# A two-attention, two-expert-layer kernel on Trainium2: the score pairs for the row maxima lead the exponentials by 36 heads in place of 28

## The chip, the cores and the metric

The kernel runs on one core of one Trainium2 chip. The metric is the device time of one execution in microseconds (us), as the median of several. All work of the core is done by TensorE (PE, matrix products), VectorE (DVE), ScalarE (ACT), GpSimd (POOL) and the DMA engines, which the queue of SyncE (SP) feeds here. Each of them has an instruction stream of its own, written by hand, and they meet at semaphores: an instruction that waits holds up everything behind it in its own stream, and nothing else.

## The reference, cut to what matters

The model applies four residual layers to x, which is 16 batches of 128 tokens by 256 features: a cross-attention with 16 heads of 8 features, an expert layer with 64 experts, an mLSTM-like attention, and a transformer block with its own attention and four experts. Only the first is touched:

```
q = split_heads(layernorm(x)^T @ Wq^T + bq)      # 16 batches, 16 heads, 256 positions, 8 features
k = split_heads(ctx^T @ Wk^T + bk)
v = split_heads(ctx^T @ Wv^T + bv)
attn = softmax(q @ k^T / sqrt(128))               # 256 x 256 for each batch and head
out = attn @ v, heads joined, @ Wo^T + bo
x = x + tanh(g_xattn[0]) * out
```

Positions are the 256 features of x, and the 128 tokens are what the projections mix. So there are 16 x 16 = 256 heads in all, counted through from batch 0, head 0.

## The kernel before, in words

The first attention is `layer0_attention`, with one function for each engine. The projections come first, two batches at a time. Each projected q and k is cut into three bf16 parts, written to HBM (L132), and read back as a "stack" of one batch: `a_qs` holds 72 rows (9 part pairs of 8 features) by 16 heads by 256 positions, `a_ks` the same for the keys. A product over these 72 rows gives a score of nearly fp32 accuracy. `stack(b)` of `layer0_sp` (L135) issues the six DMAs of one batch, three for q (L146) and three for k (L147), of 192 KB each. The stacks lie in a ring of `A_RING` = 4, so stack b + 4 overwrites stack b, and before it is issued SP waits until PE is through with the exponentials' pairs of batch b (L144). Stacks 0 to 3 are loaded with no such wait.

Each head is multiplied twice. `score_max` (L195) makes the scores with the queries on the partitions (two matmuls, L204), and DVE reduces them to the negated row maxima (L423). When a batch's 16 heads are reduced, `max_to_rows` turns the 128x32 tile of maxima with a transpose (L214), ACT copies it (L327, L328), POOL cuts it into three bf16 parts (L474 to L478), and SP writes these as three more rows of the query stack with three small DMAs (`max_rows`, L150 to L154). Then `exponentials` (L223) makes the scores again with the keys on the partitions, now over 75 rows, so that the maximum is already subtracted (L232), and ACT takes the exponential (L340). For every four heads `times_v` (L246) multiplies by v and by ones, `normalise` turns the sums back (L256), and once a batch `to_features` and `residual` (L265, L270) do the output projection.

The order of the work is a loop over `A_STEPS` steps of two heads, the same in every engine's function. Ahead of it, PE runs `AHEAD` heads of `maxima` alone. In the loop, head i of the exponentials is preceded by head i + `AHEAD` of the maxima (L278). The transpose of a batch's maxima follows two heads behind the batch's last head (L218 to L220). ACT (L350 to L355) and DVE (L437 to L445) follow the same count. SP's stream is in L162 to L171: first the max rows that fall into the first `AHEAD` heads, then a loop over the steps that issues `max_rows` where the count reaches a batch's end, and `stack` at the end of each eighth step. SP does not compute, so its loop only fixes an order; each entry goes when its own semaphore allows it and all entries ahead of it are gone.

With `AHEAD` = 28, `max_rows(0)` is issued ahead of the loop. In it the order is `max_rows(1)` (step 2), `stack(4)` (step 7), `max_rows(2)`, `stack(5)`, `max_rows(3)`, and so on. PE needs stack 4 at head 64 of the maxima, which stands ahead of head 36 of the exponentials, and turns the maxima of batch b ahead of exponentials' head 5 of batch b - 1.

Of the kernel before, what the change touches and what calls it, by code (L numbers as in the profile page):

```python
# [71 lines left out]
HEADS, HD = 16, 8  # L72
# [9 lines left out]
A_SLOTS = 3  # L82
A_RING = 4
A_EXPS = 8
AHEAD = HEADS + 3 * HEADS // 4
A_STEPS = NB * A_PAIRS + 6


# [23 lines left out]
def layer0_sp(k, m, s, ring):  # L112
# [22 lines left out]
    def stack(b):  # L135
        r, i = b % A_RING, b // 2
        flat = lambda t, first, count: t[first * HD:(first + count) * HD, :, :].rearrange("p h n -> p (h n)")
        parts_of = lambda n: io[f"a_{n}_parts"][b].rearrange("t (d h) n -> t d (h n)", d=HD)
        sp.wait_ge(ring["q_out"][i % A_SLOTS], 2 * DMA * (i // A_SLOTS + 1))
        sp.wait_ge(ring["k_out"][i % A_SLOTS], 2 * DMA * (i // A_SLOTS + 1))  # L140
        if b < A_RING:
            sp.wait_ge(s.k_ones, b + 1)
        else:
            sp.wait_ge(s.exp_scores, (b - A_RING + 1) * HEADS)  # L144
        for t in range(3):
            sp.dma_start(flat(m.qs[r], 3 * t, 3), parts_of("q")[t].unsqueeze(0).broadcast_to([3, HD, HEADS * POS])).then_inc(ring["stack_in"][r], DMA)  # L146
            sp.dma_start(flat(m.ks[r], 3 * t, 3), parts_of("k")).then_inc(ring["stack_in"][r], DMA)  # L147
# [12 lines left out]
    for b in range(1, A_RING):  # L160
        stack(b)
    for i in range(AHEAD):  # L162
        if i >= 2 and (i - 2) % HEADS == HEADS - 1:
            max_rows((i - 2) // HEADS)
    for n in range(A_STEPS):
        for h in range(2):
            i = 2 * n + h + AHEAD - 2
            if i % HEADS == HEADS - 1 and i // HEADS < NB:
# [5 lines left out]
def layer0_pe(k, m, s, ring):  # L174
# [41 lines left out]
    def maxima(i):  # L216
        if i < NB * HEADS:
            score_max(*divmod(i, HEADS))  # L218
        b, h = divmod(i - 2, HEADS)
        if h == HEADS - 1 and 0 <= b < NB:  # L220
            max_to_rows(b)
# [50 lines left out]
    pe.wait_ge(k.ident_ready, 1)  # L272
    for i in range(AHEAD):
        maxima(i)
    for n in range(A_STEPS):
        b, j = divmod(n, A_PAIRS)
        for h in (2 * j, 2 * j + 1):
            maxima(b * HEADS + h + AHEAD)  # L278
            if b < NB:
# [11 lines left out]
def layer0_act(k, m, s, ring):  # L291
# [38 lines left out]
    def maxima(i):  # L330
        b, h = divmod(i - 2, HEADS)
        if h == HEADS - 1 and 0 <= b < NB:
            max_to_rows(b)
# [15 lines left out]

    for i in range(AHEAD):  # L350
        maxima(i)
    for n in range(A_STEPS):
        b, j = divmod(n, A_PAIRS)
        for h in (2 * j, 2 * j + 1):
            maxima(b * HEADS + h + AHEAD)  # L355
            if b < NB:
# [1937 lines left out]
```

## Time and profile before

| what | us |
|---|---|
| median of 3 runs | 1828.59 (1820.28 to 1829.84) |
| the profiled execution's own time | 1817.43 |
| its span | 1816.1 |
| PE busy, share of the span | 1606.5 (88%) |
| DVE busy | 1259.6 (69%) |
| ACT busy | 1019.4 (56%) |
| POOL busy | 765.8 (42%) |
| projections and first stacks | 0 to 111 |
| loop of the first attention | 111 to 350.4 |
| the other three layers | 350.4 to 1816.1 |

An engine's busy time is the sum of its instructions' times; PE's is modelled at the ends of matmuls, so a busy PE need not be at its peak. The last three lines come from the timeline of instructions: the first exponential pair starts at 110.93, and the first layer's last residual ends at 350.4. The granted clock of a stretch is given as a share of TensorE's full speed: 1.00 is 2.4 GHz, 0.50 is 1.2 GHz.

### The profile page before, as it was taken

The numbers are of one execution on the slowest core, as the hardware profiler recorded it, in microseconds if no ns is written. First come the engines' busy times: TensorE is split into PE (matmuls) and PEld (weight loads), VectorE is DVE, ScalarE is ACT, GpSimd is POOL, SyncE is SP. The second block draws the span as 40 slices with busy tenths as digits, with TensorE's granted clock in tenths as the row PEclk, the third lists the DMA queues.
The fourth block names the chain that finished last, engine by engine and source line by source line (L and its number), as shares of the span: only waits on it lengthen the run. The fifth ranks groups of instructions, "written<-read, shape, count | busy, mean of one in ns | idle before, by whom it ended". The sixth has DMA issues, their size and how long they took to land.

```text
span 1816.1 us, 30483 instructions
## 1 busy us (share of the span) xinstructions
PE 1606.5 (88%) x10932; PEld 1268.4 (70%) x10932; DVE 1259.6 (69%) x2321; ACT 1019.4 (56%) x2050; POOL 765.8 (42%) x575
## 2 busy tenths in 40 slices
PE   4379999789999999999986964899899999999898
PEld 2135555368888888888872533788787778888687
DVE  6458788378644455444445576999999999999454
ACT  4247777644433335333335653877776877677453
POOL 5200000024435333333330014798798688877000
PEclk9569899899999999999996987999999999999899
DMA  5613232243343333343400002123112111211220
GB/s 155 154 55 83 76 84 61 80 111 105 94 129 106 104 110 102 108 116 102 118 10 6 4 2 92 48 72 103 56 56 68 56 56 56 68 48 30 70 47 24
DMA packets 73349, 137.42 MB, mean 76 GB/s; under 512 B 12824, under 2 KB 41308, under 8 KB 70384
## 3 DMA queue, kind: packets, MB, share of 16 engines
q1 hardware_dynamic: 73200, 135.48, 26.4%
q8 instruction: 88, 1.44, 0.3%
q14 instruction: 61, 0.50, 0.1%
HBM read 125.70 MB, written 8.95 MB: 74 GB/s over the span
## 4 chain that ended last, share of the span: by engine, by line
PE 54%; DVE 19%; issue 9%; DMA 8%; ACT 6%; POOL 2%; SPq 1%; DVEq 0%; ACTq 0%; POOLq 0%
PE bank L67 13%; PE bank L69 13%; PE bank L68 13%; DMA a_qs<-a_mparts 5%; DVE b_straight L1938 3%; DVE b_straight L1892 2%; PE bank L246 2%; PE bank L232 2%; PE bank L204 2%; ACT b_turned L1809 2%; DVE b_peak L1909 2%; POOL e_hidden L944 1%; DVE b_probs L1907 1%; PE bank L1700 1%; PE bank L1732 1%
## 5 line engine op out<-in xcount | busy, mean ns | idle before, releaser
L944 POOL TENSOR_TENSOR e_hidden<-e_gated,e_comb_wide 128x512 f32<-128x512 f32 x132 | 211.0, 1599 | 346.7 <-DVE e_gated L909 331.1
L784 ACT CAST e_hidden_hi<-e_hidden 128x512 fp32r<-128x512 f32 x132 | 82.0, 622 | 320.6 <-POOL e_hidden L944 320.6
L902 DVE TENSOR_TENSOR e_hidden_lo<-e_hidden,e_hidden_hi 128x512 fp32r<-128x512 f32 x132 | 98.2, 744 | 209.8 <-ACT e_hidden_hi L784 209.8
L423 DVE TENSOR_REDUCE a_negmax<-bank 128x2 f32<-128x512 f32 x256 | 165.6, 684 | 64.6 <-PE bank L204 63.3
L69 PE MATMUL bank<-e_x_hi,e_weights_lo 128*128 128x512 f32 (+1 forms) x528 | 209.5, 397 | 0.0
L67 PE MATMUL bank<-e_x_hi,e_weights_hi 128*128 128x512 f32 (+1 forms) x528 | 208.4, 395 | 0.7 <-ACT e_comb_rows L744 0.7
L68 PE MATMUL bank<-e_x_lo,e_weights_hi 128*128 128x512 f32 (+1 forms) x528 | 208.4, 395 | 0.0
L1809 ACT ACTIVATE b_turned<-bank,b_swap_bias 64x512 f32<-64x512 f32 x256 | 174.9, 683 | 17.7 <-PE bank L69 12.9
L1996 POOL TENSOR_TENSOR b_turned<-b_turned,b_rope 128x512 f32<-128x512 f32 x128 | 167.5, 1329 | 5.3 <-ACT b_turned L1809 4.8
L340 ACT ACTIVATE a_exp<-bank 128x512 f32<-128x512 f32 x256 | 142.9, 596 | 42.8 <-PE bank L232 35.4
L69 PE MATMUL bank<-e_weights_hi,e_hidden_lo 128*128 128x256 f32 (+1 forms) x528 | 149.4, 283 | 0.0
L67 PE MATMUL bank<-e_weights_hi,e_hidden_hi 128*128 128x256 f32 (+1 forms) x528 | 148.2, 281 | 0.5 <-DVE e_hidden_lo L902 0.5
L68 PE MATMUL bank<-e_weights_lo,e_hidden_hi 128*128 128x256 f32 (+1 forms) x528 | 148.4, 281 | 0.0
L1938 DVE TENSOR_TENSOR b_straight<-b_straight,b_turned 128x512 f32<-128x512 f32 x128 | 140.5, 1136 | 0.0
L1798 ACT ACTIVATE b_probs<-b_probs,b_peak_scaled 128x128 f32<-128x128 f32 x256 | 99.7, 391 | 68.2 <-DVE b_peak_scaled L1911 68.1
L204 PE MATMUL bank<-a_ks,a_qs 72*128 72x256 bf16 x512 | 108.0, 297 | 31.0 <-DMA a_ks<-a_k_parts 13.2
L1978 POOL TENSOR_TENSOR b_qk_lo<-b_raw_qk,b_qk_hi 128x512 fp32r<-128x512 f32 x64 | 84.7, 1324 | 109.9 <-DVE b_qk_hi L1872 109.9
L909 DVE TENSOR_TENSOR e_gated<-e_silu,bank 128x512 f32<-128x512 f32 x132 | 90.5, 686 | 56.7 <-PE bank L69 44.2
L232 PE MATMUL bank<-a_qs,a_ks 75*128 75x256 bf16 x512 | 100.2, 280 | 21.0 <-DMA a_qs<-a_mparts 20.1
L69 PEld LDWEIGHTS bank<-e_x_hi,e_weights_lo 128*128 128x128 f32 (+1 forms) x528 | 98.7, 187 | 22.7
L67 PE MATMUL bank<-b_x_hi,b_qk_hi 128*128 128x512 f32 x256 | 103.0, 402 | 12.8 <-POOL b_qk_lo L1978 4.5
L67 PEld LDWEIGHTS bank<-e_x_hi,e_weights_hi 128*128 128x128 f32 (+1 forms) x528 | 99.4, 188 | 19.7 <-ACT e_comb_rows L744 1.1
(326 smaller groups left out, 4318.1 us busy)
## 6 DMA issues: line engine op xcount, KB each, us to landing
e_comb_wide<-e_combT SPq DMA_DIRECT2D x130, 256.0 KB, 4.0
e_raw<-in_e_weights SPq DMA_DIRECT2D x64, 384.0 KB, 4.5
b_raw_qk<-in_b_wqk SPq DMA_DIRECT2D x64, 256.0 KB, 2.8
a_qs<-a_q_parts SPq DMA_DIRECT2D x48, 192.0 KB
a_ks<-a_k_parts SPq DMA_DIRECT2D x48, 192.0 KB
b_raw_v<-in_b_wv SPq DMA_DIRECT2D x16, 512.0 KB, 3.8
b_raw_o<-in_b_wo SPq DMA_DIRECT2D x64, 128.0 KB, 2.0
moe_comb_wide<-b_comb_rows SPq DMA_DIRECT2D x16, 256.0 KB, 6.7
```

Of the source, the lines that this page charges most:

```text
L67: pe.matmul(out, w_hi, x_hi, start=start, stop=False, skip_group_check=True)
L68: pe.matmul(out, w_hi, x_lo, start=False, stop=False, skip_group_check=True)
L69: return pe.matmul(out, w_lo, x_hi, start=False, stop=stop, skip_group_check=True)
L204: last = pe.matmul(bank[:, qb * POS:(qb + 1) * POS], m.qs[r][0:TERM_ROWS, h, qb * P:(qb + 1) * P], m.ks[r][0:TERM_ROWS, h, :], start=True, ...
L232: last = pe.matmul(bank[:, kb * POS:(kb + 1) * POS], m.ks[r][0:ROWS, h, kb * P:(kb + 1) * P], m.qs[r][0:ROWS, h, :], start=True, stop=True)
L340: act.activation(m.expo[at % A_EXPS][:, :, :].rearrange("p k q -> p (k q)"), banks[2 + h % 2][:, :], ACT.Exp, scale=float(1 / np.sqrt(np.f ...
L423: dve.tensor_reduce(m.negmax[b % 2][:, h, :], banks[h % 2][:, :].rearrange("p (q n) -> p q n", q=2), AX.X, ALU.max, negate=True).then_inc( ...
L944: pool.tensor_tensor(m.hidden[i][0:rows, :], m.gated[i][0:rows, :], m.comb_wide[u % E_RING][0:rows, chunk * BANK:(chunk + 1) * BANK], ALU. ...
L1798: last = act.activation(w.probs[n % 3][:, b, :], w.probs[n % 3][:, b, :], ACT.Exp, scale=SCALE, bias=w.peak_scaled[i][:, b:b + 1], accum_o ...
L1809: last = act.activation(w.turned[i][dst:dst + half, which, :], banks[bank][src:src + half, :], ACT.Identity, bias=m.swap_bias[dst:dst + ha ...
L1938: dve.tensor_tensor(w.straight[n % 2][:, which, :], w.straight[n % 2][:, which, :], w.turned[n % 2][:, which, :], ALU.add).then_inc(s.rotated)
L1996: pool.tensor_tensor(x, x, w.rope[:, 1, :].unsqueeze(1).to_broadcast([P, CHUNK, S]), ALU.mult).then_inc(s.qk_sine)
```

## The change

One constant:

```
-AHEAD = HEADS + 3 * HEADS // 4
+AHEAD = 2 * HEADS + HEADS // 4
```

`AHEAD` goes from 28 to 36. PE, ACT and DVE now run 36 heads of the maxima ahead of the loop, and exponentials' head i is preceded by maxima head i + 36; the last 36 exponential heads have no maxima beside them, where it was 28. `max_rows(0)` and `max_rows(1)` are issued by SP ahead of its loop. In the loop the order becomes `max_rows(2)` (step 6), `stack(4)` (step 7), `max_rows(3)`, `stack(5)`, and so on. PE needs stack 4 ahead of exponentials' head 28, which is head 12 of batch 1. The maxima of batch b are turned ahead of exponentials' head 13 of batch b - 2. The rings, tiles, instructions and waits stay as they are, as does their number.

## Rows read from the trace of the kernel before

**Rows 1.** Window: its length; busy (instructions) of PE, PEld, DVE, ACT, POOL; clock; DMA; GB/s.
```profile
125.70:323.00 197.30, 187.18 (x1871) 111.90 (x1869) 157.40 (x333) 152.19 (x319) 14.50 (x39) 0.97 0.28 75
```

**Rows 2.** Waits of PE, 90 to 620 us: total us, times, longest.
```profile
PE bank L232 <- DMA a_qs<-a_mparts: 20.1, 11, 10.0
PE bank L204 <- DMA a_ks<-a_k_parts: 13.2, 1, 13.2
```

**Rows 3.** Waits of PE, 125 to 323 us.
```profile
PE bank L232 <- DMA a_qs<-a_mparts: 10.1, 10, 2.1
```

**Rows 4.** Timeline of SP's queue: start, us, what is issued.
```profile
125.74 0.74 SPq L146 DMA_DIRECT2D a_qs<-a_q_parts  x1
...
139.57 0.76 SPq L146 DMA_DIRECT2D a_qs<-a_q_parts  x1
...
146.82 1.83 SPq L153 DMA_DIRECT2D a_qs<-a_mparts  x3
...
218.39 0.75 SPq L146 DMA_DIRECT2D a_qs<-a_q_parts  x1
```

**Rows 5.** Windows around the transfers of stacks 4 and 10 (last two: DMA share, GB/s).
```profile
128.00:131.50 3.50, 3.50 (x37) 2.09 (x37) 2.82 (x6) 2.90 (x8) 0.67 (x2) 1.00 0.71 157
131.50:135.00 3.50, 3.50 (x38) 2.10 (x37) 2.82 (x6) 2.85 (x6) 0.45 (x2) 1.00 0.24 76
...
139.50:140.50 1.00, 0.45 (x4) 0.11 (x2) 0.97 (x4) 0.61 (x2) 0.00 (x0) 1.00 0.01 2
...
232.00:232.50 0.50, 0.50 (x5) 0.18 (x3) 0.50 (x2) 0.50 (x2) 0.00 (x0) 1.00 0.03 3
```

**Rows 6.** Timeline of PE at full clock, batches 0 and 2: start, us, matmuls.
```profile
123.07 0.39 PE L204 MATMUL bank<-a_ks,a_qs 72*128 72x256 bf16 x2
...
139.56 0.39 PE L204 MATMUL bank<-a_ks,a_qs 72*128 72x256 bf16 x2
140.91 0.39 PE L232 MATMUL bank<-a_qs,a_ks 75*128 75x256 bf16 x2 [0.97 <-DMA a_qs<-a_mparts]
...
143.93 0.38 PE L204 MATMUL bank<-a_ks,a_qs 72*128 72x256 bf16 x2
...
144.67 0.28 PE L214 MATMUL bank<-ident,a_negmax 128*32 128x128 f32 x1
...
151.18 0.38 PE L204 MATMUL bank<-a_ks,a_qs 72*128 72x256 bf16 x2
...
153.86 0.39 PE L232 MATMUL bank<-a_qs,a_ks 75*128 75x256 bf16 x2
...
154.32 0.39 PE L204 MATMUL bank<-a_ks,a_qs 72*128 72x256 bf16 x2
```

**Rows 7.** Timeline of PE around its longest wait in the loop.
```profile
198.18 0.39 PE L204 MATMUL bank<-a_ks,a_qs 72*128 72x256 bf16 x2
200.70 0.61 PE L232 MATMUL bank<-a_qs,a_ks 75*128 75x256 bf16 x2 [2.13 <-DMA a_qs<-a_mparts]
...
206.03 0.64 PE L204 MATMUL bank<-a_ks,a_qs 72*128 72x256 bf16 x2
...
207.31 0.42 PE L214 MATMUL bank<-ident,a_negmax 128*32 128x128 f32 x1
...
209.92 0.61 PE L204 MATMUL bank<-a_ks,a_qs 72*128 72x256 bf16 x2
...
218.38 0.39 PE L204 MATMUL bank<-a_ks,a_qs 72*128 72x256 bf16 x2
```

**Rows 8.** Window behind that wait.
```profile
200.20:210.40 10.20, 9.70 (x60) 4.83 (x61) 3.85 (x7) 4.72 (x10) 1.11 (x3) 0.50 0.34 99
```

**Rows 9.** Timeline of the loop's end: exponential heads 228 and 246, last residual.
```profile
322.88 0.39 PE L232 MATMUL bank<-a_qs,a_ks 75*128 75x256 bf16 x2
...
336.68 0.61 PE L232 MATMUL bank<-a_qs,a_ks 75*128 75x256 bf16 x4
...
349.93 0.48 DVE L451 SCALAR_TENSOR_TENSOR resid<-a_proj,gates,resid 128x256 f32<-128x256 f32 x1 [3.05 <-ACT a_proj L369]
```

## The prediction

> **What bounds the kernel now.** Only the first attention's loop is touched, 111 to 350.4 us, so I read its window first. From 125.7 to 323 us PE is busy for 187.2 of 197.3 us, DVE for 157, ACT for 152; the DMA engines carry 75 GB/s at a mean share of 0.28 [rows 1]. PE is the bound there, short of 10 us. The list of waits says what these are: ten times PE stood before an exponential pair (L232) for the max rows' DMA, 10.1 us together, 2.1 at the longest [rows 3]. An eleventh, 10.0 us, is the one ahead of the first exponential, and before that PE waits once, 13.2 us, for a key stack [rows 2].
>
> That the max rows are late is worth a second look, because they are tiny. The reader is to see in SP's timeline that their DMAs (146.82) go out behind the six large ones of a stack (139.57) [rows 4]. The windows show what these large ones do: 157 GB/s at a share of 0.71 for some 3.5 us, then only 75 GB/s at 0.24, which is some four of 16 engines, for 8 us more, and traffic stops near 139.5 to 140.5 for stack 4, issued at 125.74 [rows 4, 5]. The max rows queued behind it release PE at 140.91 [rows 6]. Stack 10 is issued at 218.39 and its traffic has all but ended at 232 [rows 4, 5]. So a stack takes 13.6 us (232.0 less 218.4) to 15.2 us (140.91 less 125.74) from issue to use; I take 14.3, what it takes to the middle of the window 139.5 to 140.5. That is about as long as a whole batch takes on PE: from 139.56 to 154.32 is 14.8, less 1.1 of wait, 13.6 us [rows 6]. The DMA path of the stacks is nearly as full as PE, although the mean share of 0.28 hides it. This decides the case, since no stack is waited for in the loop today.
>
> **The change, part by part.**
>
> *The lead over the max rows.* The transpose of a batch's maxima comes eight heads earlier against the exponentials that need it, 19 heads ahead in place of 11. With 13.6 / 16 = 0.85 us a head that is 6.8 us more, against waits of 2.1 at most [rows 3]: all ten go, 10 us. With them goes the low clock behind the longest. That wait is 200.70 - 198.18 - 0.2 = 2.3 us, the clock granted behind it is 0.50 (1.2 GHz) from 200.2 to 210.4 [rows 8], and this batch lasts 218.38 - 198.18 = 20.2 us, so 20.2 - 13.6 - 2.3 = 4.3 us are lost to the clock [rows 7]. Together some 14 us.
>
> *Eight more heads ahead of the loop.* They fall into PE's wait of 10.0 us before the first exponential [rows 2], which ends with the landing of max rows 0, issued ahead as before; eight score pairs cannot take more than eight whole heads of the loop, 6.8 us. Were stack 2, which the last four need, late by more than the 3 us left, its lateness would be added. At the other end eight heads leave the loop at 0.85 us and are done alone at (336.68 - 322.88) / 18 = 0.77 [rows 9]: about 0.7 us gained, inside the sum below. The transpose of the maxima now follows the output projection (L270) by one head and waits for ACT to have copied it from the same bank; that costs at most a few tenths a batch, and lies inside the next wait.
>
> *The stacks' deadline.* Stack b + 4 may be issued only after exponentials' head 15 of batch b, in both kernels. Its first use was 20 heads later and is now 12. At full clock 12 heads are 151.18 - 139.56 - 1.1 = 10.5 us [rows 6], where the transfer wants 14.3. A wait of nearly 4 us is new, in each batch, on L204. Being in PE's stream, it also holds the exponential pairs behind it, then ACT and `times_v`, hence head 15 and the issue of the next stack: the wait closes a loop.
>
> *SP's order.* `max_rows(b + 2)` now stands immediately ahead of `stack(b + 4)` in SP's stream, and its maxima are turned at head 13. From head 12's score pair to the transpose are 144.67 - 143.93 = 0.74 us, from there through ACT and POOL to SP 146.82 - 144.67 = 2.15, and the three issues take 1.83 [rows 4, 6]. So the stack goes out 4.8 us behind head 12, where head 15 would allow it at 154.32 - 151.18 = 3.1 [rows 6]. Push: 1.7 us. The max rows themselves are small and don't slow the stack by more than I can read.
>
> **The sum.** With the wait in the loop, a batch lasts from one stack's landing to the next: head 12 to stack issue, plus 14.3. At full clock that is 4.8 + 14.3 = 19.1. But the wait is then 19.1 - 13.6 = 5.5 us, more than the one behind which the clock fell [rows 7, 8]. At 1.2 GHz a head's two pairs take 0.85 ((207.31 - 206.03) / 3 = 0.43 a pair), from head 12 to head 14 it is 209.92 - 206.03 = 3.9 us and the end of head 15 comes 2.0 later, at 5.9 [rows 7]; the push is hidden (1.28 + 2.2 + 1.8 = 5.3). The batch is 5.9 + 14.3 = 20.2. PE's work in it is 13.6 + 4.3 = 17.9, so 2.3 us of wait stay, just what made the clock fall before: the low clock keeps itself alive. I take 20.2.
>
> Start: batch 0 runs as now, with head 13 at 123.07. Plus 0.2 to the transpose, 2.15, 1.83 and a tenth: stack 4 goes out at 127.4 (now 125.74) and lands at 141.7. Stacks 5 to 15 are eleven periods: 11 x 20.2 = 222.2, so stack 15 lands at 363.9, at head 12 of batch 12. Behind it are 16 heads with maxima, 17.9 us, then 36 heads alone: the present end from head 228, 350.4 - 322.9 = 27.5, plus 8 x 0.77 = 6.1 [rows 9]. 363.9 + 17.9 + 27.5 + 6.1 = 415.4, against 350.4: **65 us more**. What follows the first attention starts from its last residual and does not change. From the profiled execution's 1817.4 that gives 1882; the timed runs shown lie 3 to 12 us above that execution, so I put the forecast at 1886.
>
> **A rule that speaks against it.** The rows show a transfer at 157 and then 75 GB/s [rows 5]. The Trainium skill, "DMA: Bandwidth & Descriptors" (Specifications), puts the HBM limit of one core at about 358 GB/s. By it 1.18 MB would take an estimated 3.3 us, and the stack would be there in time; the rows contradict it for these patterns. The same page (Rules for kernel authors) says that an outermost dimension smaller than 16 confines a DMA to that many engines. The key loads have an outermost 3, so it speaks for a rate that does not recover when the queue is otherwise free. No row shows which engines carried them.
>
> **Rivals.**
> (a) Faster: a stack is quicker once no max rows mix into its tail, and lands within 10.5 - 1.7 = 8.8 us. For it: the two do share the tail now. Against: traffic in the tail is 75 GB/s over 8 us, 600 KB, and three max rows are 24 KB. Then the gains alone count: 1817.4 - 14 - 1 = 1802. The page's HBM limit would lead here. 4%.
> (b) In between: transfers near 10 us, period 14.8, as now: within 0.5%. 3%.
> (c) The wait without a lasting low clock: period 19.1. 141.7 + 210.1 + 13.6 + 33.6 = 399.0, 49 us more: 1866. The clock window of a 2.3 us wait is one case only. 25%.
> (d) My forecast, 20.2: 1886, 65%.
> (e) The order on SP hurts more than computed, for instance because the large issues back up the queue, or the transfer takes 15.2 throughout: 11 x 21.1 more, 76 us: 1893, with the spread of the runs 1905. 3%.
> That the constant does nothing is excluded; it moves instructions in four streams.
>
> **Range and chances.** Lowest: transfer 13.6, full clock: 141.0 + 11 x 18.4 + 47.2 = 390.6, 40 us more, 1857. Highest: (e), 1905. Slower by over 0.5% (what a measurement of this kernel can tell from no change, 9 us): 0.93; within: 0.03; faster: 0.04.
>
> **What would show it.** In the changed kernel PE's waits should list L204 on the DMA of `a_ks` or `a_qs` twelve times, some 2 to 6 us each, and L232 on `a_mparts` once. SP should issue the first q load of a stack 1.9 us behind the first max row, and one such set each 19 to 20.5 us. The clock should be 0.50 for about half of each batch from 142 us on. The attention's end should stand near 415. Wrong it is if stacks land in under 10.5 us, or if the waits of L204 are on anything but a stack; the step I trust least is whether the low clock returns in every batch.

## The result, and the profile after

| | before | after |
|---|---|---|
| median, us | 1824.43 (1818.83 to 1829.84, 4 runs) | 1889.78 (1879.73 to 1901.54, 4 runs) |
| profiled execution, us | 1817.43 | 1886.72 |
| its span | 1816.1 | 1885.4 |
| end of the first attention in it | 350.4 | 416.9 |
| mean granted clock | 0.94 | 0.921 |

The ratio is 1.0377 (95% interval 1.033 to 1.0425): the change makes the kernel 65 us slower. Of the 69.3 us between the two spans, 66.5 lie in the first attention. The other 2.8 come behind it, in layers whose instructions are the same; single executions of one kernel differ by more than that, and I looked no further.

PE's waits from 125 to 420 us, in the kernel after (us in total, times, longest), answer to [rows 3]:

```profile
PE bank L204 <- DMA a_ks<-a_k_parts: 52.9, 12, 6.0
...
PE bank L214 <- ACT a_proj L369: 0.4, 1, 0.4
```

The ten waits for max rows are gone, and twelve waits for a stack stand in their place, one for each of stacks 4 to 15. The second line is the transpose behind the output projection. Over 90 to 430 us, as in [rows 2], one wait for max rows is left, the one ahead of the first exponential: the eight moved heads have eaten 5.7 of its 10.0 us.

```profile
PE bank L204 <- DMA a_ks<-a_k_parts: 65.5, 13, 12.7
...
PE bank L232 <- DMA a_qs<-a_mparts: 4.3, 1, 4.3
```

SP's queue after (start, us, what goes out), beside [rows 4]. The reader is to see the pair that repeats: three max rows, then at once a stack, and the next pair some 20 us on.

```profile
125.41 0.74 SPq L146 DMA_DIRECT2D a_qs<-a_q_parts  x1
...
144.18 1.84 SPq L153 DMA_DIRECT2D a_qs<-a_mparts  x3
146.54 0.76 SPq L146 DMA_DIRECT2D a_qs<-a_q_parts  x1
...
207.15 1.83 SPq L153 DMA_DIRECT2D a_qs<-a_mparts  x3
209.25 0.75 SPq L146 DMA_DIRECT2D a_qs<-a_q_parts  x1
...
352.62 0.75 SPq L146 DMA_DIRECT2D a_qs<-a_q_parts  x1
```

PE's side of it, the first score pairs of stacks 4, 5, 7 and 15, with the idle time before them in brackets, and what follows stack 7's:

```profile
140.69 0.61 PE L204 MATMUL bank<-a_ks,a_qs 72*128 72x256 bf16 x2 [6.03 <-DMA a_ks<-a_k_parts]
...
162.20 0.61 PE L204 MATMUL bank<-a_ks,a_qs 72*128 72x256 bf16 x2 [3.11 <-DMA a_ks<-a_k_parts]
...
203.66 0.61 PE L204 MATMUL bank<-a_ks,a_qs 72*128 72x256 bf16 x2 [4.69 <-DMA a_ks<-a_k_parts]
...
204.91 0.42 PE L214 MATMUL bank<-ident,a_negmax 128*32 128x128 f32 x1
...
208.77 0.39 PE L232 MATMUL bank<-a_qs,a_ks 75*128 75x256 bf16 x2
...
367.25 0.61 PE L204 MATMUL bank<-a_ks,a_qs 72*128 72x256 bf16 x2 [4.05 <-DMA a_ks<-a_k_parts]
```

From landing to landing it is (367.25 - 140.69) / 11 = 20.6 us. Of this, 15.0 us are the transfer, from a stack's issue to its first pair (mean of the twelve, 13.9 to 15.7), and 5.6 the way from that pair to the next stack's issue (mean of eleven, 5.4 to 5.85). From the score pair at 203.66 the transpose comes 1.25 later, SP's max rows 2.24 after that (207.15), head 15's pair at 208.77 ends at about 209.2, and the stack goes out at 209.25: at low clock the order on SP and the end of head 15 arrive together. The windows of the same stretch (length, PE, PEld, DVE, ACT, POOL busy, clock, DMA share, GB/s) show the low clock come with one wait and return with the next:

```profile
188.30:201.90 13.60, 10.67 (x109) 6.40 (x107) 9.73 (x22) 9.32 (x18) 0.00 (x0) 1.00 0.30 84
201.90:208.80 6.90, 5.14 (x32) 2.54 (x33) 2.02 (x3) 2.19 (x6) 1.12 (x3) 0.51 0.04 11
208.80:222.40 13.60, 11.03 (x111) 6.62 (x109) 10.04 (x23) 9.74 (x19) 0.00 (x0) 1.00 0.31 83
222.40:229.30 6.90, 4.33 (x28) 1.99 (x29) 1.38 (x2) 1.95 (x5) 1.11 (x3) 0.51 0.04 14
```

In short windows over the whole loop each of the waits for stacks 5 to 15 has such a stretch of 6.8 to 6.9 us. The first wait, 6.0 us for stack 4, has one of 13.7 us, from 137 to 150.7.

### The profile page after: what moved, and what is told of

It is laid out like the page before. It is cut to its first block, busy times and chain, and to the rows that moved or that the text cites. A ratio compares the mean times of both kernels' runs of the same rounds, so it can differ in the third digit from the quotient of the medians.

```text
span 1885.4 us, 30483 instructions
## 1 busy us (share of the span) xinstructions
PE 1638.1 (87%) x10932; PEld 1279.0 (68%) x10932; DVE 1259.6 (67%) x2321; ACT 1024.0 (54%) x2050; POOL 767.7 (41%) x575
## 4 chain that ended last, share of the span: by engine, by line
PE 57%; DVE 15%; DMA 11%; issue 7%; ACT 5%; SPq 3%; POOL 2%; DVEq 0%; POOLq 0%; ACTq 0%
PE bank L67 14%; PE bank L69 13%; PE bank L68 13%; DMA a_ks<-a_k_parts 8%; DVE b_straight L1938 3%; PE bank L1700 2%; PE bank L1732 2%; PE bank L246 2%; DVE b_straight L1892 2%; PE bank L204 2%; SPq L146 2%; PE bank L232 1%; POOL e_hidden L944 1%; ACT b_turned L1809 1%; DVE b_peak L1909 1%
## 5 line engine op out<-in xcount | busy, mean ns | idle before, releaser
L204 PE MATMUL bank<-a_ks,a_qs 72*128 72x256 bf16 x512 | 118.9, 323 | 86.0 <-DMA a_ks<-a_k_parts 65.5
L204 PEld LDWEIGHTS bank<-a_ks,a_qs 72*128 72x128 bf16 x512 | 41.5, 106 | 149.0 <-DMA a_ks<-a_k_parts 70.8
L474 POOL TENSOR_TENSOR a_mrow<-a_mrow,a_mparts 32x128 f32<-32x128 f32 x16 | 6.7, 419 | 296.8 <-ACT a_mparts L328 296.8
```

The lines of the kernel that those rows point to most:

```text
L204: last = pe.matmul(bank[:, qb * POS:(qb + 1) * POS], m.qs[r][0:TERM_ROWS, h, qb * P:(qb + 1) * P], m.ks[r][0:TERM_ROWS, h, :], start=True, ...
```

## The experiments

All are compared with the kernel before, on the same chip as itself. Ratios are to it. Except where said, each starts from the changed kernel (1.0377).

**A fifth stack slot.** The tiles of slot 4 lie in memory that the first attention does not use (`spare` stands last in the lists of `qs` and of `ks`); stack 4 is issued behind max rows 0, so that these are not held up more than needed.

```
-A_RING = 4
+A_RING = 5
...
+    spare = lambda rows, half: k.columns[0:rows, half, :].bitcast(BF16).rearrange("p (h n) -> p h n", h=HEADS)
...
-    for b in range(1, A_RING):
+    for b in range(1, A_RING - 1):
         stack(b)
...
             max_rows((i - 2) // HEADS)
+            if i // HEADS == 1:
+                stack(A_RING - 1)
```

> Five stack slots in place of four, the lead stays at 36. Stack b + 5 may then be issued after exponentials of batch b and is first used 28 heads later, as far as the max rows before the change had room. Theory (the deadline of the stack): with 28 heads, some 24 us, against a transfer of 15 us the wait of L204 on the key stacks goes, with its low clock, and so does the old wait of L232 on the max rows; time 1800 to 1815, below the kernel before. Rival (the longer lead is itself the cost: more heads outside the loop, the transposes colliding with the output projection): time stays near 1885. Rival (the stacks' transfer is too slow at any depth, a period of 15 us at least): near 1825.

Measured: 1816.45 us, ratio 0.9967 (0.9944 to 0.9991). Between 125 and 330 us the list of PE's waits has nothing of a DMA, and the window of the loop says the same (compare [rows 1]):

```profile
PE bank L217 <- ACT a_proj L372: 0.4, 1, 0.4
PE bank L235 <- ACT a_exp L343: 0.3, 2, 0.2
```

```profile
125.00:323.00 198.00, 197.01 (x1985) 115.71 (x1983) 159.18 (x343) 165.44 (x342) 15.58 (x42) 1.00 0.25 69
```

A lead of 36 is thus no loss in itself, and with the room for it PE is busy for the whole window at full clock. Both rivals fall. The time is just above the expected range because 6.5 us are lost ahead of the loop: the first exponential starts at 117.4, where it was 110.9. Two things add up to this. POOL clears the fifth key slot too, 3.65 us from 15.50 on, and everything behind comes later by about as much, up to max rows 0 (out at 98.8 in place of 95.0). From there to the first exponential it is 18.6 us in place of 15.9, with stack 4 issued just behind those rows. In the loop itself the kernel is 13.5 us quicker than the one before: the first attention ends at 343.4, where it was 350.4.

**The key loads as 24 rows.**

```
-  sp.dma_start(flat(m.ks[r], 3 * t, 3), parts_of("k")) ...
+  sp.dma_start(flat(m.ks[r], 3 * t, 3), io["a_k_parts"][b].rearrange("t (d h) n -> (t d) (h n)", d=HD)) ...
```

> Lead 36, but the key stack is read from HBM as 24 rows instead of 3 by 8 rows: the same bytes to the same places. Theory: the key loads run on few engines because of their outermost 3; with 24 rows the tail at 75 GB/s goes, a stack lands in some 8 us in place of 15, inside the 10.5 us that 12 heads give; L204 no longer waits and the time is 1800 to 1815. Rival: the shape as written does not decide (the query loads with the broadcast are the slow ones, or both shapes are the same to the engines): transfers stay at 15 us and the time at 1890.

Measured: 1885.58 us, 1.0349 (1.0313 to 1.0386). The theory's view of the keys fell; twelve waits, 55.2 us, are all there, and a stack takes 14.5 to 15.6 us as before.

**A lead of 32, and one of 34.** `AHEAD = 2 * HEADS`, and `2 * HEADS + HEADS // 8`.

> Lead 32, halfway. The stack is used 16 heads behind its issue, and the next stack is issued ahead of that use, so the wait no longer holds up the issue of the next stack. Theory (closed loop): the penalty needs the use to stand within the batch behind the issue by less than a transfer; at 16 heads, 13.6 us, against 15, the wait is 1 to 2 us, the period 14.5 to 15.2, the time within 10 us of the kernel before (1815 to 1835). Rival (a longer lead costs by the head, or the deadline alone counts, 2.5 us of it a batch being lost with the clock): half of the change's loss, about 1855.

> Lead 34. The stack is used at head 14 behind its issue, so still within the batch that must end before the next stack may go, and SP still has max rows b + 2 ahead of stack b + 4. Theory (closed loop): it is a cliff between 32 and 34. From head 14 to the transpose 1.3 us at low clock, 2.2 to SP, 1.8 for the three issues: the stack goes out 5.4 us behind the landing of the one before, the period is 15.0 + 5.4 = 20.4, as with 36; time 1875 to 1890. Rival (what counts is only how many heads of time the transfer has, two more than with 36): 2 heads, 1.7 us a batch, 20 us less, 1865. Rival (halfway between 32 and 36): 1855.

Measured: 32 gives 1821.97 us, 0.9991 (0.9968 to 1.0015); 34 gives 1887.83 us, 1.0367 (1.0306 to 1.0428). The whole loss lies in two heads. PE's waits, with 32 (125 to 350 us):

```profile
PE bank L204 <- DMA a_ks<-a_k_parts: 8.4, 6, 1.8
PE bank L232 <- DMA a_qs<-a_mparts: 0.3, 2, 0.2
...
```

and with 34 (125 to 420 us):

```profile
PE bank L204 <- DMA a_ks<-a_k_parts: 46.5, 12, 5.9
...
```

With 32, stack b + 4 is first needed when exponentials' head 15 of batch b + 1 is through. That head is what allows stack b + 5 to go, so its issue stands ahead of the wait and is not held by it. With 34, heads 14 and 15 of batch b + 1 stand behind the wait, and the period is (371.21 - 146.31) / 11 = 20.4 us. The rivals, a cost by the head or by the transfer's shortage, wanted 1855 to 1865 there.

**The order on SP.** `stack(b + 4)` ahead of `max_rows(b + 2)`:

```
-    for n in range(A_STEPS):
-        ...
+    for b in range(NB):
+        if b + A_RING < NB:
+            stack(b + A_RING)
+        if b + 2 < NB:
+            max_rows(b + 2)
```

> Lead 36, SP issues stack b + 4 ahead of max rows b + 2 and no longer behind them. Theory: the max rows push the stack only at full clock; in the changed kernel the clock is low behind each wait and the end of head 15 comes about as late as the third max row's issue, so the gain is 0 to 0.5 us a batch, 0 to 5 us in all: 1880 to 1890. Rival (the order on SP is what costs, 1.7 us or more a batch): 20 us less, 1865 or below.

Measured: 1884.5 us, 1.0352 (1.0314 to 1.0389), in the expected range. From landing to issue it is 5.45 us on average, where it was 5.6: the order is nearly hidden behind the low clock.

**Work in the wait.** Ahead of the wait for stacks 4 to 15:

```
+        if h == 0 and b >= A_RING:
+            pe.wait_ge(s.maxed, at - 1)
+            for _ in range(48):
+                pe.matmul(bank[:, 0:POS], m.qs[(b - 1) % A_RING][0:TERM_ROWS, 0, 0:P],
+                          m.ks[(b - 1) % A_RING][0:TERM_ROWS, 0, :], start=True, stop=True)
```

> Lead 36; ahead of each wait for stacks 4 to 15 PE multiplies 48 pairs of an older stack's rows into the bank that the score pair then overwrites, some 5 us at full clock, so that it works through most of the wait. Nothing of the result changes. Theory (transfer plus head 12 to issue): without the low clock head 12 to issue is 4.8 us in place of 5.6, set by the max rows ahead of the stack on SP, so the period falls from 20.6 to 19.8 and the end is 2 to 3 us quicker: 8 to 13 us less, 1874 to 1882. Rival (the low clock carries most of the loss): 1840 or below. Rival (PE's own work bounds the batch): the time rises by twelve times 5 us.

Measured: 1880.03 us, 1.0297 (1.0243 to 1.0352). Two of PE's stack waits in its timeline, with the clock at 0.99 over 125 to 400 us (0.84 in the changed kernel):

```profile
142.97 0.39 PE L208 MATMUL bank<-a_ks,a_qs 72*128 72x256 bf16 x2 [0.90 <-DMA a_ks<-a_k_parts]
...
362.58 0.39 PE L208 MATMUL bank<-a_ks,a_qs 72*128 72x256 bf16 x2 [0.56 <-DMA a_ks<-a_k_parts]
```

The period is (362.58 - 142.97) / 11 = 19.96, where 19.8 was expected, and the first attention ends at 409.2, 7.7 us sooner. From landing to issue it is now 4.85 us, the transfer still 15.1. The low clock has a share of the loss, but a small one: PE has time to spare in the batch. The profiled execution as a whole was no quicker (span 1887.2), the other layers having taken 10 us more in it; the ratio is the firmer number.

**Both.** Work in the wait, and the stack ahead of the max rows on SP.

> The same matmuls through the wait, and stack b + 4 ahead of max rows b + 2 on SP. Theory: at full clock the order on SP is what holds the stack, 1.7 us a batch, which the low clock hid when the order alone was turned; the period falls to 15.0 + 3.1 = 18.1, that is 2.5 us times eleven less than the changed kernel and 1.7 less than the one with the matmuls alone: 1855 to 1865. Rival (SP's order never mattered): the same time as the matmuls alone.

Measured: 1868.07 us, 1.0247 (1.0186 to 1.0308), 398.0 at the end of the first attention, 3 us above the range. The interval overlaps that of the matmuls alone, so it is the trace that tells the two apart. The issues of stacks 4 and 5, in SP's queue:

```profile
126.19 0.74 SPq L146 DMA_DIRECT2D a_qs<-a_q_parts  x1
...
145.22 0.76 SPq L146 DMA_DIRECT2D a_qs<-a_q_parts  x1
```

They are 19.0 us apart, not 18.1, and PE no longer waits for any DMA in the loop: with 48 matmuls of 0.11 us its own work is 13.6 + 5.3 = 18.9, so the aid has become the bound. The order on SP is therefore worth at least 19.96 - 19.0 = 1.0 us a batch at full clock, and nothing at low clock; that it is 1.7 is not shown.

**Nine query loads.** Each broadcast load of 24 rows becomes three loads of 8 rows; the waits count to 12 in place of 6.

```
-  sp.dma_start(flat(m.qs[r], 3 * t, 3), parts_of("q")[t].unsqueeze(0).broadcast_to([3, HD, HEADS * POS])) ...
+  for copy in range(3):
+      sp.dma_start(flat(m.qs[r], 3 * t + copy, 1), parts_of("q")[t]) ...
```

> Lead 36; each query load, 8 rows read three times by a broadcast, becomes three loads of 8 rows: nine loads of 64 KB in place of three of 192 KB, the key loads as they are. Theory, after the key loads' shape was shown not to decide: the broadcast's outermost 3 keeps the query loads on three engines and they are the tail at 75 GB/s. Spread out, the tail goes, a stack lands 8 to 10 us behind its issue (nine more issues of 0.45 us in place of three of 0.74), inside the 8.8 to 10.5 us it has; time 1800 to 1820. Rival (the tail is in the keys, or in the reading of HBM): transfers of 15 to 17 us, time 1885 to 1905.

Measured: 1880.99 us, 1.0312 (1.0259 to 1.0366): far from the 1800 to 1820 of the theory, and 4 us below the rival's range. The kernel with the key loads as 24 rows issued stack 4 at the same time (127.40, against 127.39 here), so that windows can be laid side by side. That one first, then this one:

```profile
131.50:135.00 3.50, 3.50 (x37) 2.11 (x36) 2.82 (x6) 2.84 (x6) 0.00 (x0) 1.00 0.39 105
135.00:139.50 4.50, 1.65 (x14) 1.15 (x11) 2.11 (x5) 2.15 (x5) 0.00 (x0) 0.97 0.19 78
```

```profile
131.50:135.00 3.50, 3.50 (x37) 2.11 (x36) 2.82 (x6) 2.84 (x6) 0.00 (x0) 1.00 0.78 103
135.00:139.50 4.50, 1.64 (x13) 1.15 (x11) 2.11 (x5) 2.14 (x5) 0.00 (x0) 0.89 0.49 86
```

So the shape of the query loads does decide how busy the engines are, but the transfer stays at 142.40 - 127.39 = 15.0 us for stack 4 and falls only from 15.0 to 14.4 on average: the engines are busier and carry little more.

**The same, with five slots.**

> Five slots, lead 36, and the nine query loads. In the loop PE already stood nowhere with five slots, so faster loads can only help ahead of it, where PE waits 13.5 us for stack 1 and 7.0 us for max rows 0. If the query loads are the slow ones: 5 to 15 us below the five-slot kernel, 1800 to 1812. If they are not: equal to it, 1816, or a few us more for the longer issue.

Measured: 1811.02 us, 0.9944 (0.9914 to 0.9974). This is the quickest whole kernel of the study, though its interval overlaps that of the five slots alone, so the times do not show what the nine loads add. The traces do, ahead of the loop: PE waits 9.5 us for stack 1 in place of 13.5, and the first exponential comes at 113.3 in place of 117.4. In the loop no stack is waited for either way.

**One kind of load left out.** The key loads, and in another kernel the query loads, of stacks 4 to 15 are left out, and the count of the wait follows. PE then works on the keys, or the queries, of the stack that lay in the slot before.

```
+            if b < A_RING:
                 sp.dma_start(flat(m.ks[r], 3 * t, 3), parts_of("k"))
```

> Lead 36; the key loads of stacks 4 to 15 are left out (the keys of stacks 0 to 3 are used again), so each of these stacks is three query loads, 590 KB in place of 1.18 MB. Theory: the transfer's length is what the wait is made of. Half the bytes land in 6 to 9 us, inside the 8.8 to 10.5 us that 12 heads give; L204 does not wait in the loop, period 13.6, time 1795 to 1812. Rival (the length is a fixed delay of the queue or of the small max rows): 1885.

> Lead 36; the query loads of stacks 4 to 15 are left out and the key loads stay. If the two kinds are alike, the same as without the key loads, 1795 to 1812. If the broadcast queries are the tail, the keys land in 4 to 5 us and the windows show no stretch at 75 GB/s; if the keys are, it stays, 8 us long.

Measured: without the key loads 1822.68 us, 1.0006 (0.9968 to 1.0044); without the query loads 1803.13 us, 0.9896 (0.9841 to 0.995). The same two windows of each, the queries alone first:

```profile
128.00:131.50 3.50, 3.50 (x37) 1.94 (x36) 3.02 (x8) 2.78 (x6) 0.00 (x0) 1.00 0.22 89
131.50:135.00 3.50, 3.46 (x34) 2.08 (x34) 2.76 (x7) 3.06 (x6) 0.00 (x0) 1.00 0.18 77
```

```profile
128.00:131.50 3.50, 3.50 (x38) 2.09 (x36) 3.02 (x7) 2.71 (x7) 0.00 (x0) 1.00 0.62 159
131.50:135.00 3.50, 3.50 (x38) 2.09 (x37) 2.76 (x7) 2.99 (x6) 0.00 (x0) 1.00 0.02 5
```

The broadcast queries are the tail: 77 to 89 GB/s at a share of 0.2, where the keys run at 159 GB/s and 0.62 and are over by 131.5. Without the queries PE waits for no DMA in the loop (period 13.9 from 126.88 to 140.77 on SP). Without the keys it still does, eleven times and for 0.6 to 2.0 us, and confirms the loop in numbers, at nearly full clock:

```profile
125.73 2.22 SPq L146 DMA_DIRECT2D a_qs<-a_q_parts  x3
...
140.41 2.24 SPq L146 DMA_DIRECT2D a_qs<-a_q_parts  x3
...
155.56 2.23 SPq L146 DMA_DIRECT2D a_qs<-a_q_parts  x3
```

```profile
135.56 0.39 PE L205 MATMUL bank<-a_ks,a_qs 72*128 72x256 bf16 x2 [0.60 <-DMA a_qs<-a_q_parts]
...
150.71 0.39 PE L205 MATMUL bank<-a_ks,a_qs 72*128 72x256 bf16 x2 [1.20 <-DMA a_qs<-a_q_parts]
```

Landing to issue is 140.41 - 135.56 = 4.85, issue to landing 150.71 - 140.41 = 10.3, the period their sum, 15.15. My expectation of 6 to 9 us for half the bytes was short, as was the 1795 to 1812 with it. The theory of the loop stands, with the 4.8 that the prediction had for full clock. That the loss goes with the transfer's length is shown by both; the wait itself is gone only without the queries.

**Both shapes.**

> Lead 36; nine query loads of 8 rows and key loads of 24 rows, the two changes of shape together, each of which alone left the transfer at 14 to 15 us. If each kind of load held the other in a shared queue, both have to be spread: the transfer falls to 8 to 10 us, time below 1830. If the limit is in the bytes and where they go, a rate of some 80 to 100 GB/s for 72 rows whatever the shape: transfer 12 to 15 us, time 1860 to 1885.

Measured: 1878.59 us, 1.0318 (1.0251 to 1.0386): within what the nine query loads gave alone. Why spreading the loads over more engines leaves a stack at 13.5 to 15 us is open.

## Why the prediction was right, point by point

The forecast of 1886 and the median of 1889.78 agree, as do their reasons: the stack's deadline, and the loop that the wait closes. That the end of the first attention was met so closely, 415.4 against 416.9, is in part luck. Of the terms, stack 4's issue was 2.0 us too late, its transfer 1.0 too short, the eleven periods together 4.4 too short, and what follows stack 15's landing 1.9 too long.

- *The old waits go.* Right, all ten, and they came back in none of the kernels with a lead of 36. The five slots show what that is worth: 13.5 us in the loop, near the 14 of the prediction, of which that kernel loses 6.5 again ahead of the loop. Without the query loads, where nothing is lost ahead of it, the first attention ends at 336.6, 13.8 us sooner than before.
- *Eight heads in the wait ahead of the loop.* Right: they cost nothing there.
- *Twelve waits on L204.* Right in place, number and size (3.1 to 6.0 us). I had them at 2.3 in the steady state, though; the mean is 52.9 / 12 = 4.4.
- *The period.* 20.6 in place of 20.2. The transfer, issue to first pair, was 15.28 for stack 4 (140.69 - 125.41), 15.66 for stack 5 and 14.63 for stack 15, 15.0 on average, where I took 14.3; landing to issue was 5.85 ahead of stack 5, 5.59 ahead of stack 8 and 5.6 on average, where I had 5.9. The two errors are of opposite sign and cancel in part.
- *Start and end.* Stack 4 went out at 125.4, not 127.4, mostly because this execution's first exponential came at 109.2 in place of 110.9; from stack 15's landing to the end it was 416.9 - 367.25 = 49.6, where I had 51.5, with 4.3 us of loss to the low clock in it. The next point has that loss as 2.6.
- *The low clock.* It did come back in every batch, which was the step I trusted least, but for 6.9 us in place of 10.2 (13.7 at the first wait alone), part of them within the wait itself. The batch then leaves 20.6 - 4.4 - 13.6 = 2.6 us to it, not 4.3. "About half of each batch" was wrong, a third is right. The matmuls in the wait show how little of the period this is, 0.6 us of 20.6: only the work between landing and issue is both on the path and slowed, the rest of the batch has the wait to spare.
- *The tail.* Here I followed the Trainium skill's rule on the outermost dimension to the wrong loads. By the runs without one kind, it is the broadcast queries that go at 77 GB/s, not the keys. That rule of the Trainium skill, "DMA: Bandwidth & Descriptors" (Rules for kernel authors), names a leading broadcast as its example. The queries alone, at a share of 0.18 to 0.22, that is 2.9 to 3.5 engines of 16 on average, are near the three it allows; the keys' 3 by 8 rows, at 0.62, are not, and writing them as 24 rows left the transfer as it was. No term of the sum depended on it.
- *Rivals.* (a) needed a transfer within 8.8 us and (b) one near 10; the shortest with all six loads in the changed kernel was 13.9. (c), the period without low clock, was 19.1 as computed and 19.96 as measured with the matmuls, the transfer being longer. (e), which I gave 3%, was nearer than that says: its transfer of 15.2 throughout is almost what came, and the measured 1890 lies midway between my 1886 and its 1893. It was the shorter way from landing to issue that kept the period at 20.6.

## What to carry to other kernels

A lead is bought with a ring: going further ahead moves the first use of a buffer towards the work that must end before the buffer behind it can be refilled. As long as the next refill is issued ahead of the wait, a late transfer costs its shortage; once the wait stands ahead of that issue, every round costs the transfer plus what lies between landing and issue, and the step between the two is a cliff (32 heads: nothing; 34: all of it). So before deepening a lead, count the slots and the heads between issue and first use, against a transfer time read from the trace and not from the mean DMA share, which was 0.28 here while each transfer took a batch.

## What the runs showed of the hardware that I had not expected

- Three broadcast query loads of 192 KB took 9.8 to 11.1 us from issue to use, and all six loads 13.9 to 15.7. The three key loads alone were over within 4.6 us (issued at 126.88, traffic all but gone by 131.5). Leaving out the keys thus saved about what the keys alone take: the two kinds cost as much as if they ran one after the other, and not beside each other. Why is not shown.
- With nine query loads in place of three the DMA share from 131.5 to 135 us was 0.78 in place of 0.39, and the rate 103 GB/s in place of 105. From 125 to 143 us both kernels moved 1.20 MB, in 396 packets in place of 333, and the packets' time was 43.0% of the engines' span in place of 22.7%: a packet took longer, so a higher share is not a higher rate.
- In the kernel after, the granted clock was 0.50 for 6.8 to 6.9 us around waits of 3.1 to 5.1 us and for 13.7 us around the one of 6.0; in the kernel before it was so for 10.2 us around the wait of 2.3 us [rows 8], and not at all around those up to 1.4. With the lead of 32, six waits of 0.9 to 1.8 us each had a low stretch, five of 3.4 us and one of 10.2. The length of the stretch did not follow that of the wait closely, and short waits were no safeguard.
